# One wait per head instead of three ahead of VectorE's bias pass, in the loop of a four-block transformer kernel

## What is computed

```python
x = x + _layernorm(_L0_attn_ref(_layernorm(x), Wq, Wk, Wv, Wo, bo))      # causal softmax attention, 16 heads of 64, ALiBi bias
x = x + _layernorm(_L0_ffn_ref(_layernorm(x), weight, disha))            # one matrix product
x = x + _layernorm(_L1_attn_ref(_layernorm(x), ...))                     # linear attention: products of K and V states
x = x + _layernorm(_L1_ffn_ref(_layernorm(x), ...))                      # 64 experts, top 8, capacity 160, and a shared expert
```

```python
scores = jnp.einsum('bihd,bjhd->bhij', q, k) * scale + bias[None]        # bias: slope * distance
scores = jnp.where(causal[None, None], scores, jnp.float32(-1e+30))
attn = jax.nn.softmax(scores, axis=-1)
```

## Time and profile before

| | |
|---|---|
| time, median of 3 runs | 2282.12 us (2282.05 to 2282.18) |
| time of the profiled execution | 2280.29 us |
| its span, first to last instruction | 2278.5 us |
| TensorE matmuls busy | 2193.5 us, 96% |
| VectorE busy | 1088.2 us, 48% |
| ScalarE busy | 867.4 us, 38% |
| GpSimd busy | 864.3 us, 38% |
| mean granted TensorE clock | 0.989 of full speed |
| the loop's six iterations | about 163 us each |

### The profile page before, as it was taken

The page is one execution under the profiler, slowest core; times in us unless marked ns, Lnnn a source line. Parts: engine busy times, 40 slices in busy tenths (PEclk is TensorE's granted clock), DMA queues, the critical chain, the costliest instruction groups (busy, mean ns, idle before and its releaser), DMA issues.

```text
span 2278.5 us, 37541 instructions
## 1 busy us (share of the span) xinstructions
PE 2193.5 (96%) x11764; PEld 1623.5 (71%) x11764; DVE 1088.2 (48%) x4114; ACT 867.4 (38%) x2128; POOL 864.3 (38%) x959
## 2 busy tenths in 40 slices
PE   7999999999999999999999799989999999999997
PEld 3565665665666666666666556579999999999955
DVE  3526666666665756756755544212222222222236
ACT  4656546555545655645555311111111111111110
POOL 3325535526535534534545440502322222223322
PEclk9999999999999999999999899999999999999999
DMA  9200001000000000000000320147787878788651
GB/s 328 81 10 10 1 29 53 30 28 26 10 31 21 14 22 13 21 15 13 21 8 21 118 82 10 42 148 272 255 274 251 276 255 273 254 271 261 221 166 59
DMA packets 101598, 244.69 MB, mean 107 GB/s; under 512 B 22836, under 2 KB 78355, under 8 KB 93152
## 3 DMA queue, kind: packets, MB, share of 16 engines
q1 hardware_dynamic: 75360, 223.83, 26.9%
q0 software_dynamic: 26112, 19.55, 5.4%
HBM read 193.71 MB, written 87.91 MB: 124 GB/s over the span
## 4 chain that ended last, share of the span: by engine, by line
PE 82%; DVE 10%; issue 4%; ACT 2%; POOL 1%; DMA 0%; DVEq 0%; SPq 0%; POOLq 0%; ACTq 0%
PE bank L1711 18%; PE bank L1379 10%; PE bank L1724 9%; PE bank L1414 7%; PE bank L1390 5%; PE bank L1624 5%; PE bank L1404 4%; PE bank L1633 4%; PE bank L1362 3%; PE bank L1368 3%; PE bank L1354 2%; DVE stats L865 2%; ACT prob L674 2%; PE bank L1464 1%; PE bank L1456 1%
## 5 line engine op out<-in xcount | busy, mean ns | idle before, releaser
L585 POOL TENSOR_TENSOR prob<-prob,rsum 128x128 f32<-128x128 f32 (+3 forms) x512 | 371.8, 756 | 614.0 <-DVE rsum L941 614.0
L1711 PE MATMUL bank<-pT,big_w 128*128 128x160 f32 x3072 | 441.1, 301 | 0.7 <-DVE pT L1222 0.7
L1711 PEld LDWEIGHTS bank<-pT,big_w 128*128 128x128 f32 x3072 | 425.5, 191 | 1.1 <-issue 1.1
L1379 PE MATMUL bank<-kT,qpad 128*128 128x512 f32 (+3 forms) x1024 | 347.5, 443 | 21.8 <-DVE rawmax L931 20.6
L590 POOL DMA_INDIRECT disp<-send,slot x288 | 283.2, 983 | 202.7 <-DVE slot L1126 116.8
L931 DVE CUSTOM_DVE_ANT_0 prob<-bank,dist 128x512 f32<-128x512 f32 (+3 forms) x512 | 229.9, 487 | 192.0 <-PE bank L1379 157.9
L660 ACT ACTIVATE pT<-bank 128x512 f32<-128x512 f32 (+1 forms) x384 | 201.7, 526 | 240.4 <-PE bank L1390 232.2
L643 POOL DMA_INDIRECT acc<-qpad,token_e x64 | 99.1, 1549 | 506.7 <-ACT qpad L828 219.5
L674 ACT ACTIVATE prob<-prob,negmax 128x512 f32<-128x512 f32 (+3 forms) x512 | 280.4, 550 | 4.6 <-DVE negmax L937 3.0
L821 ACT ACTIVATE pT<-bank 128x480 f32<-128x480 f32 x128 | 73.0, 570 | 469.5 <-PE bank L1711 469.5
L1379 PEld LDWEIGHTS bank<-kT,qpad 128*128 128x128 f32 x1024 | 173.2, 194 | 104.6 <-DVE rawmax L931 36.4
(11 more groups left out here) (181 smaller groups left out, 2714.1 us busy)
## 6 DMA issues: line engine op xcount, KB each, us to landing
big_w<-ew SPq DMA_DIRECT2D x64, 1536.0 KB, 7.0
big_w<-ew SPq DMA_DIRECT2D x64, 768.0 KB, 5.5
disp<-send SPq DMA_DIRECT2D x1, 10272.0 KB, 35.9
xT<-disp SPq DMA_DIRECT2D x64, 160.5 KB, 5.2
disp<-send,slot POOLq DMA_INDIRECT x288
xs<-x SPq DMA_DIRECT2D x8, 512.0 KB, 3.8
x<-x SPq DMA_DIRECT2D x8, 512.0 KB, 3.8
x_d<-x SPq DMA_DIRECT2D x8, 512.0 KB
```

What stands on the lines that cost most here:

```text
L585: i = g.tensor_tensor(pr, pr, rsum[:, n, t:t + 1].to_broadcast([P, COLS[t]]), ALU.mult)
L1379: ins = mm(bank[S_BANKS[u]][:, col:col + COLS[t]], qpad[:, hp % 2, s, t * P:(t + 1) * P], kT[:, hp % 2, 0:COLS[t]], start=True, stop=True, ...
L1711: i = mm(bank[2 * half + 1 - part][:, q * CAP:(q + 1) * CAP], w1[:, c, f * P:(f + 1) * P], xbT[:, c], start=(c == 0), stop=(c == C - 1), s ...
```

## The change

In the loop (first part of the index not None) VectorE waits once, for the third score unit of the head, and then runs the four operations; the wait ahead of each unit and the increment behind each are gone. Outside the loop the waits ahead of the units stay, without the increment.

```diff
@@ -924,9 +924,12 @@
                 if i[0] is not None or i[1] or n >= 4:
 
                     dve.wait_ge(ring_psum, ring_count(*t_unit(i if n >= 4 else before(i), n - 4)))
+                if i[0] is not None:
+                    dve.wait_ge(scores, at(i, 3 * H, 3 * n + 3))
+                    fixed()
                 for u, unit in enumerate(S_UNITS):
-                    dve.wait_ge(scores, at(i, 3 * H, 3 * n + u + 1))
-                    fixed()
+                    if i[0] is None:
+                        dve.wait_ge(scores, at(i, 3 * H, 3 * n + u + 1))
                     for t, col in unit:
                         v.tensor_tensor_reduce(
```

## The result

| | before | after |
|---|---|---|
| median of 20 executions each | 2280.8 us | **2286.47 us** |
| ratio of the times, 95% interval | | 1.0027 (1.0019 to 1.0035) |
| span of the profiled execution | 2278.5 us | 2284.1 us |
| mean granted TensorE clock | 0.989 | 0.993 |

The change makes the kernel 0.27% slower; 2289.1 us was forecast, in a range from 2283.0 to 2296.0.

What follows compares the result with a forecast made beforehand. TensorE, with a matmul in flight for 96% of the span, was taken as the bound. Delays of +12.0 us and the clock's -5.0 made +7.0, so 2287.3 profiled; with the 1.83 us offset 2289.1 us, range 2283.0 to 2296.0.

Steps and rivals of the forecast that it cites:

- Delay of a head: Bias pass on VectorE in the loop: with the single wait, a head for which VectorE was ready ends 1.30 us later.
- Place 1: Head 12: its late pass delays xn and TensorE's transposes of it, with no slack, by 1.30 us per iteration.
- Place 2: Heads 14, 15 and 0: what is left of head 14's delay lengthens TensorE's wait at head 1 by 0.54 us.
- Place 3: Head 4: its delay reaches head 5's reciprocal, GpSimd's normalisation and the next step's transposes, 0.12 us per iteration.
- The first iteration's 0.2: Heads 2 and 3, once in the first iteration: a delay like that at head 4, estimated at 0.2 us.
- Sum 12.0: All delays without the clock: 6 x (1.30 + 0.54 + 0.12) + 0.2 = 12.0 us, bounds 6.6 and 14.2.
- What is removed costs nothing: Waits and increments taken out, 192 of each in the loop: costed at nothing, bounds 1.8 us gained and nothing; outside also nothing.
- The clock, -5.0: Half-clock stretches behind the wait ahead of head 9 fall from five of seven to two, gaining 5.0 us.
- The total: Whole kernel: 12.0 - 5.0 = +7.0 us on the profiled execution, giving 2289.1 us, +0.31%.
- B: Rival: the same delays with as many half-clock stretches as now, 2294.1 us; chance 0.28.
- C: Rival: no change that can be told, 2285.8 or about 2283 us; chance 0.20.
- D: Rival: faster, half-clock stretches vanish and head 12's delay hides under the keys matmuls, 2276.0 us; chance 0.07.

Runs made afterwards that it cites:

- e1: Kernel after, but in the loop head 12 has its three unit waits back; 2283.68 us, ratio 1.0010 to the kernel before.
- e3: Kernel before, but in the loop head 12 alone waits once for its three units; 2286.82 us, ratio 1.0017.
- e2: Kernel after, but in the loop heads 12 and 14 have their unit waits back; 2284.02 us, ratio 1.0006 to the kernel before.
- g6: g1 with l1_sum and l1o_sum on VectorE moved ahead of the bias passes of heads 12 and 14; 2315.12 us on a chip running before in 2325.93.
- g7: g2 with l1_sum and l1o_sum on VectorE moved ahead of the bias passes of heads 12 and 14; 2314.95 us on a chip running before in 2325.93.
- e4: Kernel before, but in the loop units 0 and 1 share one wait and unit 2 has its own; 2283.91 us, ratio 1.0013.
- g1: Kernel before with x2 sums moved behind head 8's bias pass and TensorE's gram and t1 moved later; 2262.87 us, ratio 0.9919.
- g2: Kernel after with x2 sums moved behind head 8's bias pass and TensorE's gram and t1 moved later; 2273.22 us, ratio 0.9970 to before.
- f4: Kernel before with every unit wait and its increment doubled in the loop; 2283.98 us against 2280.1, ratio 1.0020.

## Why the prediction was right, and where it was off

- **Delay of a head, 1.30 us.** Right in size. The pass runs 1.72 us as one block (1.73 in the profile after), and place 1 is 1.30 by the distance of heads 13 and 14. The number of heads was misread: not ten but six get the full delay, and head 11 a wait of 0.43. The 76 waits of the earlier trace rows are two at each of these six in six iterations, and a few more. The sum doesn't use that number.
- **Place 1, 6 x 1.30.** Right, and e1 and e3 show that it is head 12. That there was no slack at all was read from the idle weight load in the earlier trace rows; the new 1.28 us wait stands exactly there.
- **Place 2, 6 x 0.54.** The path was right (e2: head 14's delay reaches head 1), the size 0.47, and 0.31 in one iteration: 2.7 us in place of 3.2.
- **Place 3, 6 x 0.12.** Not to be seen: the distance 6 to 7, where it would stand, grew by 0.05 in two iterations and by 0.01 or less in the others, 0.1 us in all in place of 0.7. GpSimd's wait by "a hair" was within what the modelled ends allow. The first iteration's 0.2 came as forecast (0.23, at 4 to 5).
- **Sum 12.0.** Between the marks the distances grew by 11.0 us: place 1 7.8, place 2 2.2 for the five times that it lies there, the first iteration 0.2, place 3 0.1, and 0.6 in small gaps at 2 to 3, 4 to 5 and 8 to 9 that were in no term. Place 2's sixth time, 0.5, lies behind the last mark. That makes 11.4, so the sum is close partly because those gaps stand against the terms that were too large.
- **What is removed costs nothing.** Right inside the loop: the steps of the pass are the same with and without the waits. Outside the loop the term was put at nothing as well, and there it is not quite that: ahead of head 8 of the last batch, where VectorE comes from its own norm, the gap was 0.22 us and is 0.03 without the increment, and 8 to 9 went from 7.22 to 7.03, 13 to 14 from 11.97 to 11.87. VectorE's timelines of before and after at that place:

```profile
1203.38 0.69 DVE L931 CUSTOM_DVE_ANT_0 prob<-bank,dist 128x512 f32<-128x512 f32 x1 [0.22 <-DVE vare L871]
```

```profile
1209.27 0.63 DVE L871 TENSOR_SCALAR vare<-mv 128x4 f32<-128x4 f32 x1
1209.93 0.69 DVE L934 CUSTOM_DVE_ANT_0 prob<-bank,dist 128x512 f32<-128x512 f32 x1
```

- **The clock, -5.0.** The direction was right. In the profiled execution one stretch of seven is left, not two, -6.6; over the executions it is rather three (estimate, above), about -3.3. The count was a choice between bounds, not a reading, so how near the total came is in part luck. The Trainium skill (TensorE: Matmul & The Clock Gate, section "What's actually happening") states that the monitor is free-running. By that the count hangs on where the waits fall; the runs agree, since waits of 2.2 us went without a half-clock stretch in six of seven cases after and in two of seven before.
- **The total.** +7.0 was forecast against the profiled execution; the medians give +5.67 and the spans +5.6. In the spans 1.96 us of that are the opening, which is not from the edit and was not in the sum. The loop itself grew by 4.30, where the same terms give 11.5 - 5.0 = 6.5: 0.5 less from the delays, 1.6 less from the fourth stretch. The time itself was carried from a base of 2282.12, the median of three executions; with all twenty it is 2280.8, so 1.3 us of the distance to 2286.47 is that.
- **Rivals.** B (as many stretches as now) falls with the profile after. C (within 0.2%) was near: had the last stretch vanished too, 1.65 us less, the time would have been 0.2% above before. D needed cover at xn, and there was none; g6 and g7 made such cover by other means, and then the delay at xn was gone.

## What to carry to other kernels

A wait for the last of several pieces doesn't save the waits for the others; it moves the work on them behind it, by the time of all pieces but the last. Ask it of each place by itself: which is the next thing on the other engine that hangs on this pass, and is there idle time on the waiting engine between? And where a wait ahead of the same engine switches the clock in some iterations only, compare variants with that wait gone, or the clock's luck, here 6.6 us between two profiled executions, stands in the result as if it belonged to the edit.

## What the runs showed of the hardware that I had not expected

- **Half-clock stretches were fewer where the iteration was longer.** With the 2.2 us wait unchanged, they came behind five of seven where an iteration without one takes 161.7 or 162.1 us (before, e2), four at 162.6 to 162.8 (e1, e4), and one to three at 163.6 (after, e3). With the wait gone there is none (g1, g2). f4 has four at 162.9. Each count is of one execution, and e3's executions alone show mean granted clocks from 0.990 to 0.993, so this is no more than an observation. I have no row that says why; it may be no more than where the waits fall.
- **The opening differs from run to run.** Head 0's first score matmul starts between 25.4 and 28.8 us in the fourteen traces, whose openings have the same work, and all that follows moves with it. A difference of two single spans below 3 us says nothing.
- **Small issue gaps move with the program.** A gap of 0.3 to 0.6 us on VectorE turned up in e1 to e4 at places where before and after have none, though the operations around them are the same.
- **The loop's jump back on VectorE is dear.** Ahead of head 2, where an iteration begins, VectorE does nothing for 3.2 to 3.3 us in the kernel before (335.84 to 339.15 in one iteration) and for as long in the one after; where head 2 isn't reached by a jump back, in the first iteration and in the last batch, the gap is 0.5 and 0.4 us in the kernel before. TensorE has other work for most of it and then waits 0.2 us ahead of head 3. With the waits doubled (f4) the gap is 3.7 to 4.0 us and TensorE's wait 0.82: that is the largest part of what f4 costs.
- **A wait is hidden behind an operation, not behind a dependency.** Inside a bias pass whose scores are at hand the step of 0.61 us doesn't change with none, one or two waits and increments ahead of the operation (head 13 in after, before and f4; head 0 in f4 is the one exception). Where VectorE comes from its own previous result the gap ahead of the pass is 0.03 us with the wait alone (last batch, after), 0.22 with the increment, 0.36 to 0.37 with the wait on a register's value and the increment, and 0.47 to 0.48 with two of each.
